# A hand-written order table for causal attention, planned again with the accumulator reads that follow masked maxima

## What is computed

```python
scores = jnp.einsum('bqhd,bkhd->bhqk', Q, K) / math.sqrt(D_K)
causal = jnp.tril(jnp.ones((Sx, Sx), dtype=bool))
scores = jnp.where(causal, scores, -jnp.inf)
attn = jax.nn.softmax(scores, axis=-1)
out = jnp.einsum('bhqk,bkhd->bqhd', attn, V)
...
x = x + _L0_attn_ref(xn, ...) + _L0_ffn_ref(xn, ...)
```

## Time and profile before

| | us |
|---|---|
| median of 3 runs | 2394.43 |
| the runs | 2391.33, 2394.43, 2430.84 |
| the profiled execution | 2401.85 |
| its span, first to last instruction | 2400.1 |
| the attention groups, first exponential to last | 277 to 1818 |
| mean granted TensorE clock of the span | 0.950 |

### The profile page before, as it was taken

The page is one execution under the profiler, slowest core; times in us unless marked ns, Lnnn a source line. Parts: engine busy times, 40 slices in busy tenths (PEclk is TensorE's granted clock), DMA queues, the critical chain, the costliest instruction groups (busy, mean ns, idle before and its releaser), DMA issues. The chain is left out here.

```text
span 2400.1 us, 45293 instructions
## 1 busy us (share of the span) xinstructions
PE 2243.1 (93%) x15977; PEld 1289.1 (54%) x15977; DVE 1901.0 (79%) x5771; ACT 1513.8 (63%) x3190; POOL 495.8 (21%) x405
## 2 busy tenths in 40 slices
PE   5995999999999999999999999999996796999997
PEld 2553444444444444444444444444434675999997
DVE  3552999989999999898898998998944796666664
ACT  2541388778788787787777877877782212545443
POOL 0001000120211201202001011010004304777765
PEclk9997699999999999999999998999997798999999
DMA  5998325254154352441524516335115454445541
GB/s 154 292 267 226 36 29 64 36 66 57 27 73 51 41 64 39 63 57 27 73 36 57 64 23 78 42 42 69 16 20 155 148 172 115 109 111 120 125 118 31
DMA packets 145060, 203.62 MB, mean 85 GB/s; under 512 B 61066, under 2 KB 107872, under 8 KB 136544
## 3 DMA queue, kind: packets, MB, share of 16 engines
q1 hardware_dynamic: 132576, 191.08, 40.6%
q0 software_dynamic: 12288, 10.05, 3.3%
HBM read 134.24 MB, written 71.83 MB: 86 GB/s over the span
## 5 line engine op out<-in xcount | busy, mean ns | idle before, releaser
L652 ACT ACTIVATE probs<-s_banks 128x512 f32<-128x512 f32 (+3 forms) x2560 | 1182.4, 538 | 326.3 <-PE s_banks L603 198.3
L689 DVE TENSOR_REDUCE rowmax<-m_banks 128x1 f32<-128x512 f32 x1536 | 966.2, 682 | 66.8 <-PE m_banks L614 61.4
L614 PE MATMUL m_banks<-ks,qs 48*128 48x512 f32 (+3 forms) x2560 | 827.5, 436 | 28.6 <-PEq L88 20.5
L603 PE MATMUL s_banks<-qs,ks 50*128 50x512 f32 (+3 forms) x2560 | 819.7, 429 | 15.3 <-ACT probs L652 8.1
L632 PE MATMUL v_bank<-probs,vs 128*32 128x512 f32 (+3 forms) x5120 | 619.2, 556 | 0.0
L603 PEld LDWEIGHTS s_banks<-qs,ks 50*128 50x128 f32 x2560 | 401.5, 188 | 397.6 <-ACT probs L652 359.9
L614 PEld LDWEIGHTS m_banks<-ks,qs 48*128 48x128 f32 x2560 | 415.5, 193 | 262.0 <-DVE rowmax L689 162.9
L686 DVE CUSTOM_DVE_ANT_0 unused<-m_banks,c_maskq 128x128 bf16<-128x128 f32 (+3 forms) x1024 | 466.8, 486 | 59.9 <-issue 51.8
L549 POOL CAST nparts<-negmax 128x16 fp32r<-128x16 f32 x64 | 12.6, 197 | 1190.1 <-DVE negmax L695 1190.1
L1436 PE MATMUL e_banks<-w_parts,hid_parts 128*128 128x256 f32 x1536 | 189.7, 284 | 2.2 <-DVE hid_parts L1355 2.2
L575 PE MATMUL s_banks<-c_identb,c_later_col 64*128 64x64 bf16 x1024 | 188.8, 196 | 0.0
(11 more groups left out here) (185 smaller groups left out, 1744.1 us busy)
## 6 DMA issues: line engine op xcount, KB each, us to landing
w<-in_L_ffn_fc_w SPq DMA_DIRECT2D x32, 1024.0 KB, 4.9
qs<-q_scratch SPq DMA_DIRECT2D x96, 256.0 KB, 8.3
ks<-k_scratch SPq DMA_DIRECT2D x96, 256.0 KB, 10.0
q_scratch<-parts SPq DMA_DIRECT2D x64, 256.0 KB, 4.4
k_scratch<-parts SPq DMA_DIRECT2D x64, 256.0 KB, 4.5
v_scratch<-vt SPq DMA_DIRECT2D x16, 512.0 KB, 7.7
v_in<-v_scratch SPq DMA_DIRECT2D x32, 256.0 KB, 10.9
qs<-mrows SPq DMA_DIRECT2D x512, 2.0 KB
```

The costliest lines, as they stand in the source:

```text
L603: ins = pe.matmul(bank, ks[rows, slot, h // 2, k * P:(k + 1) * P], qs[rows, slot, h // 2, q * CH + first:(q + 1) * CH], start=True, stop=n ...
L614: pe.matmul(room(("M", NM * group + n))[:, 0:width], qs[rows, slot, h // 2, t * P:(t + 1) * P], ks[rows, slot, h // 2, c * CH:c * CH + wid ...
L652: act.activation(probs[:, n % PR, 0:width], s_banks[:, (NS * group + n) % SRING, 0:width], ACT.Exp, scale=SCALE).then_inc(p_ready, 1)
L689: dve.tensor_reduce(out, scores, AX.X, ALU.max).then_inc(m_used, 1)
```

## The change

Only the table `TURNS` is replaced. As before it holds in its 40 strings each score once, 160 M and 40 V. The title's words say by what it was planned: the planner, which is no part of the kernel, now counts the accumulator reads behind masked maxima. `LEAD`, `TURN_AFTER`, the fixed steps, the rings and all instructions stay as they are.

```diff
-TURNS = ("0MM1M2MMM3VMMM", "012MV3M", "0M1M2MV3M", "0MM1M2M3M", "0VMM12M3VM", "012MMM3VM", "012MMVM3", "0MM12MM3",
-         "0MM12MVM3", "0MM1V2MM3V", "01M2MMV3", "0MMMM123MM", "0M12MV3", "0MMM1MV2MM3", "0V1MM23MV", "01MMM2V3",
-         "01MM2M3MV", "01M2MMV3M", "0M12MMM3", "0V1MMM2M3MM", "0V123MM", "0M1MM2M3MM", "0V12M3MMVM", "01MM2VM3",
-         "0MM1V2MM3", "0MVM1M23MVMM", "012MV3MMM", "01M2M3M", "0V12M3MMV", "0MM12MV3M", "01MM2MM3V", "0M12MMV3MM",
-         "0M1M2VM3", "0MM1M23MM", "012VM3M", "01VM2M3", "01M2MVM3MM", "01MMVM2M3", "0MVM12MM3M", "0VM123MV")
+TURNS = ("01MVM2MM3M", "0MM123MM", "0MV1MM23MV", "0MM12MV3", "0MMMM12M3V", "0M1M2MV3", "01M2MMM3MV", "0MM12V3M",
+         "01MM2MMM3", "0V12MMM3MVM", "01M2MV3MM", "01MM23MM", "0M12VMM3M", "0M1VM2M3VMM", "012MV3MM", "01MM23",
+         "0MM12VM3", "0M1VMM23MM", "0VM12M3MVMM", "012MV3M", "0M1M2M3MM", "0M1V2M3", "0MMVM1M2M3V", "0M1MM2VM3",
+         "0MM1M2M3", "01MM2MM3", "01VM23MM", "0VM1MM23", "0MV123MMM", "0MM12MM3V", "0MMM12VM3", "0M1MVM23M",
+         "0MVM12MM3VMM", "01M2VM3M", "0M123MM", "01V2MM3V", "0M12MMV3", "01MVMM2MMV3", "0MMMM12MMMM3", "0MV1MM2V3MM")
```

## The result

| | before | after |
|---|---|---|
| median, us (4 runs each) | 2398.84 | 2539.62 |
| lowest to highest | 2391.33 to 2430.84 | 2527.20 to 2549.04 |
| the profiled execution | 2401.85 | 2542.82 |
| mean granted TensorE clock | 0.950 | 0.899 |

The changed kernel is slower: the ratio is 1.056, with a 95% interval of 1.052 to 1.061. That is about 141 us; the forecast was 2387 and the range ended at 2438. Of the experiments further down, e1 and e7 have two executions each that lie 1.5% and 8% apart: the time given is that of the faster one, the trace that of the slower one.

What follows compares the result with a forecast made beforehand. VectorE was taken as nearest to the bound, tied to TensorE and ScalarE by order and rings. From 2369 us without slow stretches, less 19 for feeding, plus 37 for the clock, came 2387 us; the range was 2345 to 2438.

Steps and rivals of the forecast that it cites:

- What bounds the kernel: Attention stage: nothing saturated alone; VectorE nearest, 88.28 busy of 94.35 us a group, tied to TensorE and ScalarE.
- Term 1: Feeding of VectorE and ScalarE in each group: 1.2 us a group, 19 us gained; bounds 50 us gained, 14 lost.
- The walk over steps: Maxima work minus exponential work per step: shortfalls of 5.8 us a group old, 4.2 new; 1.7 us gained.
- The second walk: From one P V to the next, larger of VectorE's and TensorE's work: 90.3 us old, 91.2 new, 0.9 worse.
- Term 2: TensorE's clock in turns 36 to 37 and 22 to 23: falls in 12 of 16 groups, 37 us lost; bounds 0 to 74.
- Rival (a): Whole attention stage: feeding improves and the clock stays up, 2350 us, or 2337 with 2 us a group; chance 0.17.
- Rival (c): Clock falls in every group at the end and again around steps 24 to 26, 2443 us; chance 0.13.
- Rival (b): Masked maxima: accumulator reads cost 10 ns, not 83, so no gain in clean groups and as many falls, 2394 us; chance 0.20.
- The rule of the Trainium skill: TensorE between matmul groups: short idle spells as banks cycle swing its clock between half and full rate; 74 us by it alone.
- Moves costed at nothing: SP, POOL, loads, row stores and ScalarE's copies: shifts cost nothing, covered by 10 or more us of distance.

Runs made afterwards that it cites:

- e1: Changed table's order of scores and maxima, with the products V put back where the old table has them: 2652 us, 1.10 of the kernel before.
- e7: Changed table's scores and maxima, with one product in every step, behind score 2: 2574 us, 1.07 of the kernel before.
- e14: Kernel before with one 128-row, 128-column TensorE product added ahead of every tenth maxima product, 16 a group: 2501 us, ratio 1.040.
- e9: Changed table with 16 TensorE products added per group, ahead of the maxima products of steps 24, 25 and 38: 2626 us, ratio 1.097.
- e13: Kernel before with a one-column VectorE write added ahead of each unmasked maximum, 96 a group: 2412 us, ratio 1.003.
- e3: Steps 0 to 10 of the changed table joined to steps 11 to 39 of the old: 2480 us, ratio 1.032.
- e15: Table of e6 with 4 score banks and 3 maxima banks in place of 3 and 4: 2569 us, ratio 1.069.
- e16: Changed table with 4 score banks and 3 maxima banks in place of 3 and 4: 2696 us, ratio 1.121.
- e10: Table of e5 with three maxima moved from step 38, two to step 8 and one to step 36: 2478 us, ratio 1.032.
- e6: Old table with only product 17 moved, from the head of step 19 to step 18: 2373 us, ratio 0.989.
- e5: Changed table with product 37 moved from step 39 to 38 and product 23 from step 26 to 25: 2485 us, ratio 1.034.

## Why the prediction was wrong, point by point

- **What bounds the kernel.** This is the step that failed first. I took VectorE as nearest to the bound and put TensorE's 93.06 busy us of 94.35 aside as a modelled number. e14 and e9 show that TensorE's row has no room for a product of full height: in e14 the whole 8.0 us was paid while VectorE idled for 13.5. e13, which was to clear VectorE by itself, added nearly nothing to it. The view that could have told it was at hand: the last group of the kernel before carries 72 of the 160 maxima, VectorE is busy for 39.5 us in it, and it still takes 91.6 of 94.4 us. VectorE is not out of it everywhere: in the turn after product 36 of the new table it holds TensorE up at 1626.65 and 1627.25.
- **Term 1, feeding: 19 us gained, measured 44 us or more lost.** The walk over steps weighed maxima against exponentials, that is VectorE against ScalarE, and so measured a shortfall that did not tell the time: by it the new table was 1.6 us a group better, and its clean group is some 3 us longer. The second walk, from one P V to the next, had the right sign (0.9 us worse) and lies nearer to what binds, but I halved it, and it was mis-sized: it took 0.1 to 0.15 us for a short product, so at most 1.85 us for a turn with six, while the earlier trace rows had 1.90, and turns with four or five short products take 1.8 to 1.9 as well (1.90 after product 5, 1.90 after 14 and 1.83 after 34 in the new table). Its worst bound, 14 us lost, did not hold the result either.
- **Term 2, the clock: 37 us in all, measured about 125** (358 us at half rate, 0.35 each by the groups of after). The mechanism and the places were right. The fall in step 18 went away with its stretch, and the turns from product 36 to 37 and 22 to 23 brought it down instead. Only the size failed: I took falls of 6.8 us and 3 us each; they lasted 13.65 us or followed each other, 12 to 29 us a group before the last. I assumed that the clock comes back as quickly as before. The upper bound of this term was 74 us. Rival (a) took step 18 for the only place where falls begin; 4 of the 13 of before begin in step 21, behind one in 18, and one in step 34 of the last group.
- **Rival (c)**, slower by the clock, had the right mechanism for two thirds of the loss, and a price of 2443 that took the same short falls. I gave it 0.13. It was set up with no loss in feeding, and the two come together.
- **Rival (b)** has some support: the plan counts 64 reads of 83 ns as VectorE's work, 5.3 us a group, and by the earlier trace rows they cost 10 ns each; the writes of e13, 5.7 us by their durations, are the same case. That the planner was misled by this is argued, since it is not part of the kernel.
- **The rule of the Trainium skill** on banks cycled with short idle spells (TensorE: Matmul & The Clock Gate, "A second HAM failure mode: psum-queue depth-cycling"), set against the change in the prediction, had the sign right: the clock swung between 0.50 and 1.00, and before the fall at 1628.2 stand two holes of 0.22 us where TensorE waits for a bank. The sum that the prediction drew from it, with 74 us for the clock, would have been 2424, still 116 us short.
- **Moves costed at nothing.** Loads, row stores, SP and POOL show no new wait. ScalarE's copies do: the 0.7 us a group in step 18, and the turn after product 17 that holds the transpose.
- **Still open**: what makes clean groups 3 us longer with the new table. 2.2 us of it come with steps 0 to 10 (e3), and the turn after product 17 may hold the rest. A fourth score bank, paid for with a maxima bank, did not help (e15, e16), and filling poor turns did not bring it back (e10). Unpaired short products are not it either, 10 a group against 12. That TensorE's row has no room is shown over the whole group for the old table only (e14), and for two turns of the new one (e9). What VectorE adds in the new one is not tested, and e13 did not load it in the old one.

## What to carry to other kernels

Where three engines are tied by an order and by rings, add a little work to each engine in turn and see which one lengthens the loop; busy shares of 94 and 99% don't tell that. Look in the trace first whether the added work reached its engine: instructions must follow each other later than before (e14), not at the same distance (e13). Read TensorE's clock by the stretch: a table that leaves it with thin, small products between two large ones can lose more by the clock than by waits, and one slow stretch can lead to the next. When a hand-tuned table is good, moving a single item at the place that the trace names can be worth more than a new plan (e6, 1.1% faster, against 5.6% slower).

## What the runs showed of the hardware

- The half rate seems to keep itself going: in e7's trace the same order ran five groups in a row at full clock, 104.1 us each, and nine of the other whole groups with 48 to 86 us at half rate in 121 to 134 us.
- A microsecond at half rate cost 0.35 us between groups of the kernel after and of e7, 0.40 in e5, and 0.45 in the kernel before (3.05 us for 6.8).
- With 16 products of 128 rows added to each group of the old table, spread evenly, the clock stayed up for 15 groups, at 8.0 us a group (e14). The same number placed in two turns of the new table left 278 us at half rate (e9). The tables differ, so this does not compare the places alone.
- A write of one column (59 ns) ahead of a maximum of 512 columns added nothing to the distance between maxima: 0.61 us with it and without (e13).
- The read of the accumulator (83 ns) runs beside the next instruction: a masked maximum of 512 columns repeats every 0.62 us, an unmasked one every 0.61.
